# Attention with an int8 gate on eight cores: K's evacuation ahead of Q's copies, half of the AV matmuls behind the V projection, three V buffers

## The reference

```python
s = attention(xn)                 # q, k, v = xn @ Wq.T, xn @ Wk.T, xn @ Wv.T; 16 heads of 64
                                  # causal sliding window of 128 keys, softmax, then @ Wo.T
g = silu(int8_matmul(xn, rhs))    # rows of xn and columns of rhs rounded to int8 by their absmax
x = x + s * g
```

## Time and profile before

| | us |
|---|---|
| median of 2 runs | 944.92 |
| the two runs | 917.45 and 972.38 |
| the profiled execution | 920.44 |
| its span, slowest core | 918.8 |
| spans of the eight cores | 901.6 to 918.8 |
| busy in the span: TensorE, VectorE, ScalarE | 682.8, 522.7, 426.6 |
| granted TensorE clock, mean over a core | 0.978 to 0.988 |

### The profile page before, as it was taken

One profiled execution on the slowest core, in us unless ns is written; L12 is line 12 of the kernel. 1 busy time (PEld: TensorE's weight loads), 2 busy tenths in 40 slices (PEclk: granted clock), 3 DMA queues, 4 the chain that ended last, 5 costly groups with the idle time before them and its releaser, 6 DMA issues.

```text
span 918.8 us, 13168 instructions; the slowest of 8 cores (901.6 to 918.8 us)
## 1 busy us (share of the span) xinstructions
PE 682.8 (74%) x4561; PEld 346.9 (38%) x4625; DVE 522.7 (57%) x986; ACT 426.6 (46%) x417; POOL 17.5 (2%) x36
## 2 busy tenths in 40 slices
PE   0000278788889888788888888878888988888873
PEld 0000134344444444344444444434444444444432
DVE  4235316566665666566666666655666666666623
ACT  0000145555544555455555555555555555555531
POOL 7000000000000000000000000000000000000000
PEclk9999999999899999999999999999999999999996
DMA  7991623434434443444444444353434444433321
GB/s 156 189 188 49 160 58 70 98 98 103 104 69 104 103 101 95 68 95 103 104 103 104 105 103 99 97 104 85 94 98 105 103 103 105 104 94 79 81 35 58
DMA packets 193041, 91.28 MB, mean 99 GB/s; under 512 B 179272, under 2 KB 179656, under 8 KB 192976
## 3 DMA queue, kind: packets, MB, share of 16 engines
q1 hardware_dynamic: 188368, 82.04, 37.3%
q0 software_dynamic: 4608, 8.39, 6.0%
HBM read 37.98 MB, written 16.78 MB: 60 GB/s over the span
## 4 chain that ended last, share of the span: by engine, by line
PE 53%; DMA 19%; ACT 15%; issue 6%; DVE 4%; SPq 2%; ACTq 0%; DVEq 0%
PE p_proj L477 38%; DMA bfp<-bfp 13%; PE p_av L576 12%; DMA scr<-rhst 6%; ACT bfp L394 4%; ACT bfp L413 4%; ACT bfp L409 4%; ACT bfp L435 2%; ACT bfp L407 2%; PE p_sc L494 2%; PE p_sc L499 2%; SPq L160 1%; DVE sm L297 1%; DVE scr L302 1%; DVE q32t L305 1%
## 5 line engine op out<-in xcount | busy, mean ns | idle before, releaser
L477 PE MATMUL p_proj<-wbf,bfp 128*128 128x512 bf16 x1473 | 346.7, 389 | 77.2 <-ACT bfp L413 46.8
L477 PEld LDWEIGHTS p_proj<-wbf,bfp 128*128 128x128 bf16 x1536 | 147.6, 100 | 246.0 <-issue 94.8
L477 PE MATMUL p_proj<-qrhs,bfp 128*128 128x512 bf16 x512 | 120.7, 378 | 30.6 <-ACT bfp L435 30.6
L576 PE MATMUL p_av<-wbf,bfp 128*128 128x512 bf16 x511 | 117.6, 384 | 5.1 <-DMA bfp<-bfp 5.1
L447 ACT ACTIVATE scr<-scr 128x1024 f32<-128x1024 f32 x32 | 33.8, 1056 | 163.7 <-DVE scr L349 163.7
L388 ACT ACTIVATE bfp<-p_sc 128x2048 bf16<-128x2048 f32 x32 | 60.1, 1877 | 57.8 <-PE p_sc L499 57.8
L477 PEld LDWEIGHTS p_proj<-qrhs,bfp 128*128 128x128 bf16 x512 | 47.7, 97 | 103.6 <-issue 54.4
L358 DVE TENSOR_TENSOR scr<-p_av,scr 128x1024 f32<-128x1024 f32 x32 | 39.2, 1225 | 75.5 <-PE p_av L576 75.5
L422 ACT ACTIVATE q32t<-scr,sm 128x1024 int32<-128x1024 f32 x32 | 36.8, 1149 | 91.6 <-DVE bfp L307 90.9
L576 PEld LDWEIGHTS p_av<-wbf,bfp 128*128 128x128 bf16 x512 | 50.6, 99 | 66.8 <-issue 7.9
L329 DVE TENSOR_TENSOR bfp<-bfp,mstd_s 128x2048 bf16<-128x2048 bf16 x60 | 71.0, 1222 | 3.6 <-ACT bfp L401 3.6
(11 more groups left out here) (57 smaller groups left out, 686.5 us busy)
## 6 DMA issues: line engine op xcount, KB each, us to landing
scr<-x SPq DMA_DIRECT2D x32, 512.0 KB, 4.4
y<-scr SPq DMA_DIRECT2D x32, 512.0 KB, 2.9
scr<-rhst SPq DMA_DIRECT2D x8, 512.0 KB
bfp<-bfp SPq DMA_TRANSPOSE x160, 3.0
wbf<-wqt POOLq DMA_DIRECT2D x8, 256.0 KB, 16.0
wbf<-wkt POOLq DMA_DIRECT2D x8, 256.0 KB, 26.4
wbf<-wvt POOLq DMA_DIRECT2D x8, 256.0 KB, 36.4
wbf<-wot POOLq DMA_DIRECT2D x8, 256.0 KB, 46.6
```

The costliest lines, as they stand in the source:

```text
L477: mms.append(lambda kc=kc, half=half: tensor.matmul(p_proj[:, half * 512:(half + 1) * 512], lhs_t[:, lhs_base + kc * 128:lhs_base + kc * 1 ...
L576: mms.append(lambda kc=kc, half=half, c=c: tensor.matmul(p_av[:, half * 512:(half + 1) * 512], bfp2[:, AOT[c % 2] + kc * 128:AOT[c % 2] + ...
```

## The change

- `VS` gets a third buffer: V of chunk c lies in `VS[c % 3]`, AVS reads `VS[c % 3]` and `VS[(c + 2) % 3]`. The initial zeros go to the third buffer, and its ones are set too.
- ScalarE: the copy of K (`kte`) goes ahead of the wait for `trq` and the two QTM copies; the copies of V (`vev0`, `vev`) go ahead of the square `sq`.
- TensorE: the second AVS group of chunk i goes behind the V projection of chunk i+1.
- Nothing is added to or taken from the work, but for one memset of 16 columns.

```diff
-VS = [10240, 11280]
+VS = [10240, 11280, 12320]
...
                 if 0 <= i + 1 < nchunk:
                     c = i + 1
+                    W(scalar, "t", ("k", c))
+                    I(lambda: scalar.copy(bfp[:, KROW:KROW + 1024], p_proj[:, 0:1024]),
+                      "a", ("kte", c))
                     Wv(scalar, f"trq{c % 2}", 16 * (c // 2 + 1))
                     I(lambda c=c: scalar.copy(bfp[0:64, QTM[c % 2]:QTM[c % 2] + 1024],
                                               bfp[0:64, QTF:QTF + 1024]))
                     I(lambda c=c: scalar.copy(
                         bfp[64:128, QTM[c % 2] + 1024:QTM[c % 2] + 2048],
                         bfp[64:128, QTF:QTF + 1024]), "a", ("qtm", c))
-                    W(scalar, "t", ("k", c))
-                    I(lambda: scalar.copy(bfp[:, KROW:KROW + 1024], p_proj[:, 0:1024]),
-                      "a", ("kte", c))
...
                     SWS(lambda c=c: scalar.activation(
                         bfp[:, QB[c % 2]:QB[c % 2] + 1024], q32[:], AF.Copy,
                         bias=-MAGIC), "a", ("qbf", c))
+                if 0 <= i + 1 < nchunk:
+                    c = i + 1
+                    W(scalar, "t", ("v", c))
+                    I(lambda c=c: scalar.copy(
+                        bass.AP(bfp, VS[c % 3], [[BFP_COLS, 128], [65, 8], [1, 64]]),
+                        bass.AP(p_proj, 0, [[1024, 128], [64, 8], [1, 64]])),
+                      "a", ("vev0", c))
...
+                if 0 <= i + 2 < nchunk:
+                    c = i + 2
                     I(lambda c=c: scalar.activation(
                         scr[:, CEN[(c + 1) % 2]:CEN[(c + 1) % 2] + 1024],
                         scr[:, CEN[c % 2]:CEN[c % 2] + 1024], AF.Square,
                         accum_out=sm[:, SQS[c % 2]:SQS[c % 2] + 1]), "a", ("sq", c))
...
                     AVS(c, 0)
-                    W(tensor, "v", ("e1m", c))
-                    AVS(c, 1)
                 if 0 <= i + 1 < nchunk:
                     c = i + 1
                     W(tensor, "a", ("kte", c))
                     if c == 0:
                         Wv(tensor, "lwv", 128)
                     PROJ(c, "v", bfp, XNT[c % 2], wbf, 2 * 8192)
+                if 0 <= i < nchunk:
+                    c = i
+                    W(tensor, "v", ("e1m", c))
+                    AVS(c, 1)
+                if 0 <= i + 1 < nchunk:
+                    c = i + 1
                     W(tensor, "a", ("vev0", c))
```

More of the change, by code:

```diff
@@ L35 @@
 KT = [8192, 9216]
-VS = [10240, 11280]
[L37 to L40, removed]
+VS = [10240, 11280, 12320]
+QTF = 13360
+QTM = [14384, 16432]
+QROW, KROW = 18480, 19504
+BFP_COLS = 20560
 ERAW = 0
@@ L228, in emit_vector @@
             I(lambda: vector.memset(bfp[:, KT[1]:KT[1] + 1024], 0.0))
-            SW(lambda: vector.memset(bfp[:, VS[1]:VS[1] + 1040], 0.0))
+            SW(lambda: vector.memset(bfp[:, VS[2]:VS[2] + 1040], 0.0))
             I(lambda: vector.memset(
@@ L232, in emit_vector @@
             I(lambda: vector.memset(
-                bass.AP(bfp, VS[1] + 64, [[BFP_COLS, 128], [65, 16]]), 1.0),
+                bass.AP(bfp, VS[1] + 64, [[BFP_COLS, 128], [65, 16]]), 1.0))
+            I(lambda: vector.memset(
+                bass.AP(bfp, VS[2] + 64, [[BFP_COLS, 128], [65, 16]]), 1.0),
               "v", ("rings", 0))
@@ L427, in emit_scalar @@
                         bias=-MAGIC), "a", ("qbf", c))
+                if 0 <= i + 1 < nchunk:
[5 more added lines that the diff above has]
+                      "a", ("vev0", c))
+                    I(lambda c=c: scalar.copy(
+                        bass.AP(bfp, VS[c % 3] + 8 * 65,
+                                [[BFP_COLS, 128], [65, 8], [1, 64]]),
+                        bass.AP(p_proj, 512, [[1024, 128], [64, 8], [1, 64]])),
+                      "a", ("vev", c))
+                if 0 <= i + 2 < nchunk:
+                    c = i + 2
                     I(lambda c=c: scalar.activation(
@@ L431, in emit_scalar @@
                         accum_out=sm[:, SQS[c % 2]:SQS[c % 2] + 1]), "a", ("sq", c))
[L432 to L443, removed]
                 if 0 <= i + 1 < nchunk:
@@ L506, in AVS @@
             def AVS(c, grp):
-                vc_ = VS[c % 2]
-                vp_ = VS[(c + 1) % 2]
+                vc_ = VS[c % 3]
+                vp_ = VS[(c + 2) % 3]
                 mms = []
```

## The result

The changed kernel takes 920.96 us in the median (918.33 at best), the kernel before 917.56 over 42 runs. The ratio is 1.0043, interval 1.0032 to 1.0054: slower by 0.4%. Where one of the times lies near 1000 us, a whole die ran at a lowered clock in that run; the ratio leaves those out. The forecast was 925. That is 1.005 of the profiled 920.44 it was worked out from, and 7.4 us above the median of the kernel before, where 3.4 came.

A forecast was written before the change was run, and what follows sets the result against it. TensorE is the backbone, held once a period by a relay of ScalarE and a transpose. From 918.8 us span, +3.1-5.2-3.3 gives 913.4; +4.9+1.5+2 gives 921.8; slowest core 923.5, 925 in time; range 905 to 945.

The forecast's parts named there:

- Is another thing later still?: Check of other paths: L576 waits 0.6 us for the ao transpose, next Q row 15.22 after K's copy, so hidden.
- the sum: Loop period from Q row to Q row: 8.35+15.84 = 24.19 us, 0.47 more than the ordinary 23.72.
- The ring through the square: The square behind V's copies delays LN2 and trxn; the next Q waits for trxn, 20 to 35 us in 30 times.
- k: The moment when ScalarE can copy K: K's end + 0.09, 8.35 us after a Q row.
- the 0.46: Time in us taken from a transpose's landing to the recorded Q row; 0.2 to 0.5 called fair.
- The gain of K's copy: kte runs 1.25 us earlier, V starts earlier, a late trq is covered; TensorE's wait falls from 46.8 to some 15 us.
- The rest of the sum: Added for this core: late trxn landings 4.9 us, late trq 1.5, uneven small waits 2; loop start +3.1.
- six bad periods: Periods of this core with a late trq, where V waits about 2.1 us more; the change takes out nearly all.
- within 2%: Measured time of the whole kernel within 2% of no change, the rest beside A and B: chance 0.70.
- A: Rival: trxn keeps its cover ahead of Q, ordinary period 23.57 or 22.9 us, total 897 us; chance 0.10.
- B: Rival: trxn takes over trq's rate of late landings, each followed by slow matmuls, total 945 us; chance 0.20.
- C: Rival: gain and loss cancel exactly, ordinary periods at 24.0 us, about 918; counted within the forecast's 0.70.

The follow-up runs named there:

- the better order: Against the kernel before: ScalarE runs kte, QTM copies, sq, V's copies, then q32, qbf. AVS ahead of V: 872.10 us, 0.947; second group behind V: 906.65 us, 0.986.

## Why the prediction was right or wrong

**The step that failed** is "Is another thing later still?". It called the late ao transpose hidden, and so put the move of the second AVS group at nothing. Put back, the group gives 4.75 us (0.5%), and the kernel then stands at 0.9997 (0.998 to 1.002) of the kernel before: what was put at nothing is as large as the whole slowdown. A second step was mis-sized: the ring's period, 24.19 us in the sum, 24.05 measured, 4.2 us too much in thirty steps.

That 925 came near 920.96 is in part luck, since these errors have opposite signs. The base adds to it: the profiled 920.44 lies 2.9 above the median of the kernel before.

*The ring through the square.* Right, and the main thing. The forecast had Q wait for trxn for 20 to 35 us in 30 steps; it was 21.7 in 25, and without the first Q 16.8 in 24. The period came to 24.04 where the sum said 24.19. The term that was over-sized is ScalarE's: the sum took 5.54 us from k to V's copy and 1.07 from there to the square. It measured 325.06-319.59 = 5.47 and 326.02-325.06 = 0.96, since the record of a copy out of PSUM ends 0.1 us after the next copy has started (320.60 against 320.50, 326.13 against 326.02). From the landing to Q's first matmul it is 0.24 us, within the 0.2 to 0.5 stated; the 0.46 was against a record that lacks the first matmul, as suspected; with it the Q row lies 8.57 and not 8.35 ahead of k, so the total does not change. Leaving out 1.6 us on VectorE moved the changed kernel 2% and the kernel before 0.6%: the ring is shown by experiment, not only read.

*The gain of K's copy.* Right in kind: the 27 us steps are gone in the changed kernel. The remaining wait was put at 15 us and measured 24.2, 0.76 a step, since one AVS group alone does not fill the time of the copy.

*"Is another thing later still?"* It had L576 wait 0.6 us for trao and called it hidden. L584's wait was 0.44 in the step shown, and hidden in that one. The sum weighed the ordinary step only, not the uneven ones, nor the end of the loop, where nothing hides it. Taken over all pairs, the AVS move costs in every order in which it was tried: 0.5% in the changed kernel, 1.5% beside K's copy alone (1.004 against 0.989), 4% in the better order, 10% alone. It nowhere pays.

*The rest of the sum*, on the slowest core. Late landings and uneven waits were put at 4.9+1.5+2 = 8.4 us and measured 6.7 in thirty steps (a mean of 24.27 against an ordinary 24.05), some half of it by the AVS move, which was not seen. The lowered clock behind a late landing, 1.7 of the 4.9, did not come in the loop, but where nothing was put: at the first Q, which took 5.98 us instead of 3.61. So the start cost 5.0 and not 3.1. One reading was off: of the six bad periods put down to a late trq, one is the period of the late trxn.

*What a measurement can tell.* I put it at 2% and gave "within 2%" the chance. With some forty runs of each kernel the interval is 0.1% wide to either side, and +0.4% is a real slowdown, which that wording could not tell from no change or from a gain.

*Rivals.* A (trxn keeps its cover, 897) is out: no step had it. B (a rush of late landings, 945) is out in the changed kernel. C (periods of 24.0, 918) comes nearest of the three, with 24.05 and 920.96. B's half about the clock is real elsewhere: in the AVS-only kernel gaps of some 2.4 us ahead of V cost 4.4%. The Trainium skill, "TensorE: Matmul & The Clock Gate", section "Why this matters for your kernels", asks for no long idle gaps between bursts; the runs agree, and show it at a gap of 2.38 us. And the Trainium skill, "DMA: Bandwidth & Descriptors", section "Rules for kernel authors", with its advice to issue early and wait late, was the right warning: both moves that made a transpose's issue later lost time.

Put together from the runs with one or two edits: K's copy first -1.1%; the square late +1% on top (0.998 to 1.000 against 0.989), where it costs 3.8% without K's copy first; AVS late another +0.5%; in all +0.4%.

## What to carry to other kernels

In a software-pipelined loop the period is that of the longest ring through all engines; lay it out with each operation's start before moving one, and ask of each operation on the ring whether its result is needed this step. The change reordered what was urgent and left the two operations that are needed only a step later (q32, qbf) in the middle of the ring; with those behind V's copies the time fell 4% below that of K's copy alone (0.947 against 0.989). When an instruction leaves a place where it only filled a gap on TensorE, price the gap too.

## What the hardware showed unexpectedly

Eight matmuls a step whose result is thrown away made a kernel 4.4% faster (1.103 to 1.0545), by keeping the granted clock at 0.99 instead of 0.95. And DMA transposes of one size, 128x1024 in bf16, landed after 2.7 to 3.4 us in most steps and after 4 to 5.5 in some, at places that moved with the order of the program.
